# From batch 1 on, Q with K, and V of two heads, by seven block products in place of eight, with column sums taken from exponentials that stay in PSUM

## The reference

```
qkv    = x @ w_qkv                        # 512 -> 3 x 16 heads x 128
scores = q @ k.T / sqrt(128)              # per batch and head, 1024 x 1024
probs  = softmax(scores)                  # over the keys
values = einsum('bhqk,bhkd->bhkd', probs, v)
out    = values @ w_o                     # 2048 -> 512
x      = layernorm(x + out)
x      = layernorm(x + ffn(x))            # routed: 32 experts, 4 per token; and a shared expert
```

## Time and profile before

| | |
|---|---|
| Median of the runs | 2727.69 us |
| Span of the profiled execution (first to last instruction) | 2723.8 us |
| Its own time beside its span | not given by itself; the median is 3.9 us above this span |
| TensorE busy | 2698.9 us, 99% |
| VectorE busy | 2196.8 us, 81% |
| ScalarE busy | 1520.8 us, 56% |
| GpSimd busy | 807.5 us, 30% |
| TensorE's granted clock | 0.999 of full speed |
| Attention | from the start to about 2157 us |

### The profile page before, as it was taken

One profiled execution on the slowest core, in us unless ns is written; L12 is line 12 of the kernel. 1 busy time (PEld: TensorE's weight loads), 2 busy tenths in 40 slices (PEclk: granted clock), 3 DMA queues, 4 the chain that ended last, 5 costly groups with the idle time before them and its releaser, 6 DMA issues.

```text
span 2723.8 us, 41944 instructions
## 1 busy us (share of the span) xinstructions
PE 2698.9 (99%) x12882; PEld 2234.4 (82%) x12882; DVE 2196.8 (81%) x3193; ACT 1520.8 (56%) x2603; POOL 807.5 (30%) x777
## 2 busy tenths in 40 slices
PE   9999999999999999999999999999999999999998
PEld 7888888888888888888888888888887778888887
DVE  6988888889888888898888888988888787433346
ACT  5655555566565566665555657655565532255434
POOL 2222222224222222342222223422221210266621
PEclk9999999999999999999999999999999999999999
DMA  3111111113111111131111112211110231378954
GB/s 120 39 36 38 36 35 35 36 34 116 35 35 35 37 40 35 48 99 37 36 35 35 35 38 66 81 35 42 35 48 14 87 120 43 113 239 254 262 147 155
DMA packets 209640, 193.52 MB, mean 71 GB/s; under 512 B 14620, under 2 KB 162076, under 8 KB 209552
## 3 DMA queue, kind: packets, MB, share of 16 engines
q1 hardware_dynamic: 199056, 180.47, 21.0%
q0 software_dynamic: 10496, 12.02, 2.3%
HBM read 166.41 MB, written 36.18 MB: 74 GB/s over the span
## 4 chain that ended last, share of the span: by engine, by line
PE 94%; DVE 4%; issue 1%; ACT 0%; DMA 0%; POOL 0%; SPq 0%; DVEq 0%; ACTq 0%
PE banks L1828 37%; PE banks L1843 25%; PE banks L1872 13%; PE banks L1750 5%; PE banks L1799 5%; PE banks L1812 3%; PE banks L1759 2%; PE banks L1853 1%; PE banks L1786 1%; DVE colsum L1372 1%; PE banks L1674 0%; PE banks L1727 0%; DVE neg_max L1358 0%; DVE val L1407 0%; DVE raws L1319 0%
## 5 line engine op out<-in xcount | busy, mean ns | idle before, releaser
L1828 PE MATMUL banks<-xt,w_sb 128*128 (+1 forms) x4608 | 1109.2, 390 | 6.5 <-DVE xt L1458 6.5
L1828 PEld LDWEIGHTS banks<-xt,w_sb 128*128 128x128 f32 x4608 | 866.7, 188 | 187.3 <-POOL w_sb L644 6.5
L986 ACT ACTIVATE rows_a<-banks,neg_max 128x1024 f32<-128x1024 f32 x512 | 573.3, 1120 | 700.8 <-DVE neg_max L1358 696.1
L1358 DVE TENSOR_REDUCE neg_max<-banks 128x1 f32<-128x1024 f32 x512 | 625.8, 1222 | 223.6 <-PE banks L1843 212.8
L1843 PE MATMUL banks<-qk 128*128 128x512 f32 x3072 | 779.4, 389 | 0.9 <-ACT rows_a L986 0.8
L1843 PEld LDWEIGHTS banks<-qk 128*128 128x128 f32 x3072 | 576.0, 188 | 122.1 <-ACT rows_a L986 2.6
L1372 DVE SCALAR_TENSOR_TENSOR colsum<-rows_a,inv,colsum 128x1024 f32<-128x1024 f32 x448 | 615.7, 1374 | 17.9
L644 POOL TENSOR_TENSOR w_sb<-raws,w_sb 128x512 fp32r<-128x512 f32 x192 | 249.1, 1297 | 660.4 <-ACT w_sb L926 660.3
L1872 PE MATMUL banks<-wo_sb,val 128*128 128x512 f32 x1536 | 372.2, 391 | 0.2
L1872 PEld LDWEIGHTS banks<-wo_sb,val 128*128 128x128 f32 x1536 | 285.9, 188 | 67.1 <-DVE y_sb L1414 7.9
L655 POOL TENSOR_TENSOR cs<-folded,cs 64x1024 fp32r<-64x1024 f32 x63 | 152.5, 2421 | 406.7 <-ACT cs L967 406.7
(11 more groups left out here) (201 smaller groups left out, 2387.1 us busy)
## 6 DMA issues: line engine op xcount, KB each, us to landing
raws<-in_w_qkv SPq DMA_DIRECT2D x192, 256.0 KB, 2.8
wo_raw<-in_w_o SPq DMA_DIRECT2D x64, 256.0 KB, 2.8
y_sb<-in_x SPq DMA_DIRECT2D x32, 256.0 KB, 3.7
raw_own<-in_w_gate SPq DMA_DIRECT2D x16, 512.0 KB
raw_own<-in_w_up SPq DMA_DIRECT2D x16, 512.0 KB
raw_own<-in_w_down SPq DMA_DIRECT2D x16, 512.0 KB
raws<-in_xT SPq DMA_DIRECT2D x25, 256.0 KB, 3.0
x_wide<-y_sb SPq DMA_DIRECT2D x24, 256.0 KB, 3.6
```

Source lines behind the costliest of these rows:

```text
L986: act.activation(ex[:, t % 2], p_s[:, t % 2], ACT.Exp, bias=neg_max[:, t % 2], accum_out=rowsum[:, t % 2]).then_inc(act_e, 1)
L1358: dve.tensor_reduce(neg_max[:, t % 2], p_s[:, t % 2], AX_X, ALU.max, negate=True)\
L1828: ins = pe.matmul(p_g[:, g % 2], w_sb[:, a, r, c], xt_part(batch_par, b, c, half * NB, NB), start=(c == 0 and (a, b) == PASSES[0]), stop=( ...
```

## The change

**Seven products.** For batches 1 to 3 the projections are taken as products of 2x2 blocks and made by seven block products in place of eight. One such product is a `unit`: 2 chunks x 3 passes = 6 matmuls. Q and K of one head are one such product (7 units, 42 matmuls, in place of 48), and V of two heads is one (42 in place of 48). Four of the seven units run on in one PSUM bank (bank 4 for Q with K); three go into another bank and are combined by ACT (`evac_u`, `evac_v`), VectorE (`add_block`) and GpSimd (`add_v`). Batch 0 is projected as before.

**Blocks from HBM.** The sums of blocks of x and of the weights have to be there in high and low. They are made once, during batch 0 (weights: `sum_t`, `hi_t_sums`, `lo_t`; `store_w`, `store_t`) and during each batch for the next (x: `sum_x`, `hi_x`, `lo_x`, `store_x_step`), written to HBM (`w_jobs`, `x_jobs`) and read back: weights by `load_units` into a ring of seven slots, x by `load_block`.

**Exponentials stay in PSUM.** `exp_here` writes them over the scores. `add_tile` reads them there, and so `scores(t)` waits for `dve_p`, that VectorE has added tile t-2, in place of `act_e`. The SBUF buffers that held them serve as float32 scratch (`e_1`, `u_2`, `e_7`, `v_e1`).

**Who does what.** `lo_val` and the low parts of three of the four Q/K blocks move to GpSimd; splitting weights goes away for batches 1 to 3. `write_x` of the first norm moves from GpSimd to ScalarE for batches 0 to 2. Column sums take two buffers in turn (`colsums`), and the fold stays on VectorE (`fold_here`).

The core of the diff (VectorE's, ScalarE's and TensorE's steps of a pair of heads):

```diff
+        def exp_here(n, t):
+
+            tau = n * T + t
+            on_act.wait_ge(dve_m, tau + 1)
+            on_act.wait_ge(dve_r, tau - 1)
+            act.activation(p_s[:, t % 2], p_s[:, t % 2], ACT.Exp, bias=neg_max[:, t % 2],
+                           accum_out=rowsum[:, t % 2]).then_inc(act_e, 1)
+
...
+        def add_block(i, base, m, which):
+
+            q = m - H
+            pos, bank, to, term = ((P2, 1 if base == 0 else 2, e_1, 1), (P5, 0, e_7, 3), (P4, 1, u_2, 2))[which]
+            on_dve.wait_ge(pe_u, units(i, base + pos))
+            on_dve.wait_ge(act_qe, 3 * q + term)
+            of = psum[:, 4 + bank]
+            if which == 1:
+                tt(to, to, of, ALU.add).then_inc(dve_qc, 1)
+            else:
+                stt(out=to, in0=of, scalar=SCALE, in1=to, op0=ALU.mult, op1=ALU.add).then_inc(dve_qc, 1)
+
...
+        def first_half(b, i):
+            n = 2 * i
+            m = n + 1
+            eighth = isinstance(i, int) and i == PB
+            for t in range(T):
+                if t == 0:
+                    add_y(i - 2, 7 if eighth else 3)
+                if t == 1 and not eighth:
+                    add_y(i - 2, 4)
+                    add_y(i - 2, 5)
+                if t == 2 and not eighth:
+                    add_y(i - 2, 6)
+                    add_y(i - 2, 7)
+                if t == 0:
+                    add_tile(b, n - 1, T - 1, colsums[1], p_s)
+                else:
+                    add_tile(b, n, t - 1, colsums[0], p_s)
+                if t == 2:
+                    add_block(i, 0, m, 0)
+                max_tile(n, t)
+                if t == 0:
+                    fold_here(n - 1, 1)
+                if t == 3:
+                    times_v(0 if eighth else b, n - 1, 1, i - 1)
+                if t == 4:
+                    add_block(i, 0, m, 1)
+                if t == 5:
...
+        def second_half(b, i):
+            n = 2 * i + 1
+            m = n + 1
+            seventh = isinstance(i, int) and i == PB - 1
+            for t in range(T):
+                if t == 0 and seventh:
+                    add_y(i - 1, 2)
+                    add_y(i - 1, 3)
+                if t == 3:
+                    add_block(i, AT_S1, m, 1)
+                if t == 4:
+                    add_block(i, AT_S1, m, 2)
+                    times_v(b, n - 1, 0, i)
+                if t == 0:
+                    add_tile(b, n - 1, T - 1, colsums[0], ex if seventh else p_s)
+                else:
+                    add_tile(b, n, t - 1, colsums[1], p_s)
+                if t >= 5:
+                    add_y(i - 1, t - 1 if seventh else t - 5)
+                max_tile(n, t)
+                if t == 0:
+                    fold_here(n - 1, 0)
+                if t == 1:
+                    add_block(i, AT_S1, m, 0)
+                if t == 4:
+                    lo_block(m, 0)
...
+        def unit(b, i, pos, block, bank, opens):
+
+            on_pe.wait_ge(in_u[RING_OF[pos % 7]], 16 * unit_loads(i, pos))
+            if isinstance(i, int) and i % PB == PB - 1 and pos >= AT_S1:
+                on_pe.wait_ge(in_xb[block], 16 * b)
+            x = xt[:, X_AT[b][block]]
+            for c in range(2):
+                for a, half in PASSES:
+                    ins = pe.matmul(psum[:, bank], w_slot[pos % 7][:, a, c], x[:, half, c],
+                                    start=(opens and c == 0 and (a, half) == PASSES[0]),
+                                    stop=(c == 1 and (a, half) == PASSES[-1]), skip_group_check=True)
+            ins.then_inc(pe_u, 1)
+
...
+        def scores(n, par, t, banked):
 
             if t == 0:
-                on_pe.wait_ge(dve_g, 4 * (n + 1))
-            on_pe.wait_ge(act_e, n * T + t - 1)
+                if banked and not (isinstance(n, int) and n < H):
+                    on_pe.wait_ge(pool_ql, 3 * (n - H + 1))
+                    on_pe.wait_ge(dve_ql, n - H + 1)
+                else:
+                    on_pe.wait_ge(dve_g, 4 * (n + 1))
+            on_pe.wait_ge(dve_p if banked and not (isinstance(n, int) and n == M - 1 and t >= 2) else act_e, n * T + t - 1)
...
+        def first_half(b, i):
+            n = 2 * i
+            eighth = isinstance(i, int) and i == PB
+            for t in range(T):
+                scores(n, 0, t, True)
+                if t < 2 and not eighth:
+                    out_tile(b, i - 2, 4 + 2 * t)
+                    out_tile(b, i - 2, 5 + 2 * t)
+                if t == SPREAD:
+                    on_pe.wait_ge(dve_y, T * (i - 1))
+                    spread(n - 1)
+                for j in {0: (P1,), 1: (P2,), 2: (P6, P7), 3: (P5,), 4: (P4,), 5: (P3,)}.get(t, ()):
+                    qk_unit(b, i, 0, j)
+                if t >= 4:
+                    v_unit(b, i, t - 4)
...
+        def second_half(b, i):
+            n = 2 * i + 1
+            seventh = isinstance(i, int) and i == PB - 1
+            end = isinstance(i, int) and i % PB == PB - 1
+            of = b + 1 if end else b
+            for t in range(T):
+                scores(n, 1, t, True)
+                for j in {0: (P1, P2), 1: (P6, P7), 2: (P5, P4), 3: (P3,)}.get(t, ()):
+                    qk_unit(of, i, 1, j)
+                if t == SPREAD:
+                    if seventh:
+                        on_pe.wait_ge(dve_y, T * (i - 1) + 4)
+                    else:
+                        on_pe.wait_ge(act_ve, evacs(i, 7))
+                    on_pe.wait_ge(dve_qc, 3 * (2 * i + 2 - H) + 1)
+                    spread(n - 1)
+                if 4 <= t < 7:
+                    v_early(of, i, t - 4)
+                if t >= 4:
+                    if t < 6:
+                        on_pe.wait_ge(dve_v, 2 * n)
+                    out_tile(b, i - 1, t if seventh else t - 4)
```

ScalarE's side, in the second pair of heads of a batch (k1), where the first norm's rows are read and written between the exponentials:

```diff
+        def second_half(b, k, i):
+            n = 2 * i + 1
+            m = n + 1
+            k1 = k == 1
+            c = 2 * (b - 1)
+            for t in range(T):
+                if t == 0:
+                    upper_cs(n - 1, colsums[0])
+                if t == 1:
+                    if not (b == 0):
+                        evac_v(i, 6)
+                    evac_u(i, AT_S1 + P1, m, 0)
...
+                if t == 7:
+                    evac_v(i + 1, 2)
+                exp_here(n, t)
+                if k1 and t < 2:
+                    read_x(c + 1, [2 + t])
+                if k1 and t == 1:
+                    write_x(c)
+                if k1 and t == 5:
+                    write_x(c + 1)
```

1142 lines of the change are left out of this document (854 added, 288 removed).

## The result

| | before | after |
|---|---|---|
| Median of the runs, us | 2726.92 (2725.06 to 2727.95) | 2831.39 (2828.43 to 2834.28) |
| Span of the profiled execution | 2723.8 | 2826.9 |
| Mean granted clock of TensorE | 0.999 | 0.987 |

The ratio is 1.0386, with an interval of 1.0371 to 1.0401: 3.9% slower. The prediction had the sign (2764) and not the size: 2831 lies 23 us above the end of its range.

A forecast was written before the change was run, and what follows sets the result against it. VectorE and ScalarE working in turn were to set the pace, hiding TensorE's saving. Ring +7, first norm +21, batch 0 +5 and transfers +3 made +36 on 2723.8: 2760 in the profile, 2764 as median; range 2710 to 2808.

The forecast's parts named there:

- TensorE's saving: Attention projections: 432 of 4608 matmuls go, 97.9 us or 4.08 a pair of heads, hidden under VectorE and ScalarE.
- the ring: VectorE and ScalarE in turn: maximum, exponential, sum, 3.89 us a tile; with extras 66.4 a pair against 66.12, +7 us.
- second head, tile 3: VectorE between maximum and sum: add_block and times_v, 0.6 + 1.2 us, 0.4 more than the room of 1.36.
- ScalarE, late casts: ScalarE between exponentials: its fullest place takes 2.9 us of 2.8, 0.1 late, some 0.3 with what waits.
- all else: Spread-to-spread time outside batch 0 and the second pairs of batches 1 to 3: +9 us of the forecast +36.
- Durations in PSUM: Sum reading PSUM taken as 1.20 us (kept 1.13 and 1.37), exponential writing it as 1.12 (kept 1.07 and 1.25).
- rival C: Sum at 1.13 us and exponential at 1.07 make pairs 64.5 us: 2718 us; chance 0.17.
- The first norm: Second pair of a batch, three times: ScalarE's reads and writes between exponentials cost 7 us each, 21; upper end 12 each.
- Batch 0, the step that failed: First 14 heads: GpSimd's sums of weights and x stretch VectorE's sums; 18 us bare, 5 taken as waiting covers it.
- Transfers: DMA: bandwidth hidden at 109 GB/s a pair; 3 us for three batch ends, without cover 10 each.
- B: TensorE stays the bound, with a tile at 3.6 us in place of 3.89: 2638 us; chance 0.10.
- D: Exponentials in place dearer at 1.25 us (50 us), or transfers late at batch ends (27 us): 2814 us; chance 0.15.

The follow-up runs named there:

- the half sum: Changed kernel with each tile's sum, from batch 1 on, over 512 of its 1024 columns, so no longer a valid layer: 2745.11 us.
- both orders: Changed kernel with, in batch 0, the column sums' low part ahead of sum_t on GpSimd and the weights' load ahead of x's store on SyncE: 2791.26 us.

## Why the prediction was right or wrong

- **TensorE's saving.** Right: 432 matmuls fewer. That it lies hidden under the ring was shown by the half sum (86 us come out). The pace before was read a little short. 33.06 us a head is a mean of 62 distances, and the first of them is 27.66, with 122 matmuls in place of 146. A steady pair took 66.30, not 66.12.
- **The ring.** Right in its mechanism and, but for the last, in its terms: 66.83 us a pair for 66.4. From the starts of VectorE's maxima between 926.82 and 993.65, what a step takes over 3.89:

| term | forecast | measured |
|---|---|---|
| first head, tile 0: fold and two add_y | 1.1 | 1.20 |
| add_block between sum and maximum | 0.6 | 0.59 |
| second head, tile 3 | 0.4 | 0.42 |
| three add_y between sum and maximum | 1.8 | 1.78 |
| ScalarE, late casts | 0.3 | 0.62, in five steps; in two of them the exponential is late |

  What TensorE's idle time is ended by I had wrong: the sum ends almost none of it (1.4 us), ScalarE's `evac_u` and `evac_v` 85 (38.0 + 35.5 + 11.2 in the waits). These stand behind an exponential, and with half a sum the pairs get shorter, so it is the ring all the same.
  That "all else" came out at +9.5 for +9 is partly luck: the ring took more than forecast, and the 3 us for transfers at the ends of the batches did not come.
- **Durations in PSUM.** The exponential in place takes 1087 ns (1118 into SBUF); the sum from PSUM 1284, the same as from SBUF undisturbed. The Trainium skill's rule for ScalarE that the prediction named (PSUM the lower-latency destination) holds, by 31 ns: 0.5 us a pair, too little for rival C. The Trainium skill's page SBUF — State Buffer ("SBUF: two separate sides") says that a VectorE operation with two SBUF inputs and a GpSimd one that reads SBUF exclude each other. The trace agrees: 105 sums with both inputs in SBUF have a mean of 1534 ns and go up to 2390 in batch 0, those with one input in PSUM stay within 1283 to 1286 in all 336 cases, beside a GpSimd that is busy for 27 of 66 us (from 1065 to 1131).
- **The first norm.** The mechanism was right and the size short: 10.4, 9.5 and 9.5 us over a steady pair in place of 7. With the writes away and the queue in order, 3.5 are left for the reads; the prediction's own numbers give 4.1 without the writes (2.5, and 7.0 - 2.6 - 2.8 = 1.6). So the writes cost 6.0 to 6.9, where it had 2.9. The step that held a read, four writes and the split came out at 4.4, 3.6 and 3.6 for 4.2. The other four writes came out at 2.7, 2.6 and 2.6 for 0.3. The prediction asked only when the next exponential comes, and this one is in time; it did not ask what else ScalarE hands to TensorE behind the writes (`evac_v`, and 3.31 us of waiting). The reload of the rows, its upper end ("12 each"), is not what cost this: in the three pairs of the changed kernel none of the four engines that compute waits for a transfer. Such waits came only when the writes had gone to GpSimd.
- **Batch 0, the step that failed.** The prediction put it thus: sums stretched by 0.09 to 0.2 us, "bare it would cost 14 x 1.3 = 18 us. I take 5". The stretch is there, and larger: from 66 to 552 the sums have a mean of 1562 ns after 1373, 0.28 us over an undisturbed one (1285). But the prediction summed what GpSimd does and what this does to VectorE, as if the load were spread evenly. It did not ask in which order GpSimd and SyncE do it. The term was 63.6 us, and the runs with nothing but orders changed took 51 of them away: a load behind six stores, a sum that waits for it, and a split that TensorE waits for queued behind this sum. 59 of the 67 us between forecast and result are this term, 8 the norm.
- **Transfers.** Bandwidth was hidden, as forecast; order was not. The late loads that the experiments moved were late by their place in SyncE's list. The stores of x in runs of 64 words, which no row had shown, stand in that list too. Where SyncE issued a transfer right behind two of them, that issue took 2.5 to 4.2 us in 12 of 12 cases; with 4.6 us or more in between, 0.35 to 0.59, in 12 of 12. The first of the four stores at 314.34 is such a one, 2.66 of the 4.92 us.
- **Rivals.** B and C are out (pairs at 66.84). D's number, 2814, was the nearest, but for neither of its reasons: exponentials in place are cheaper, and the last pairs of a batch take 66.5 us, no more than the others. That it was the nearest is luck.

## What to carry to other kernels

When a change adds work to an engine with time to spare, its share of busy time does not give the cost (GpSimd: 42% with batch 0 at +64 us, 43% with it at +13): write down what stands ahead of each instruction that the bounding engine waits for, on that engine and on the DMA queue. Loads that something waits for go ahead of stores, which wait for results themselves. And in a ring of two engines find the place where one waits for the other: work is free there up to the length of the wait (here 1.36 us), and costs its whole duration two instructions further on.

## What the runs showed of the hardware that I had not expected

- A stall can cost more than its length. After 6.83 us idle the two matmuls of `spread` took 1.01 us and the 12 behind them 4.79, with a granted clock of 0.50 from 326 to 335. After 2.67 us idle (at 721.74 in the changed kernel) 12 took 4.26, with 0.50 from 722 to 724. At full clock (2.4 GHz) 12 take 2.72, all at 1.2 GHz would be twice that. After 1.25 us idle (at 922.36) the clock stayed at 1.00, and 12 took 2.90. With the orders mended the granted clock of the stretch from 66 to 552 us rose from 0.95 to 1.00.
- SyncE's list costs time by itself. The median of its 970 issues in the changed kernel is 0.43 us. Ten stores in a row held a load back by 9.4 us (225.97 to 235.36 with both orders), while the DMA engines were busy for about half the time (0.58 from 66 to 552 us in that run). What an issue right behind two stores of x takes stands above, at the transfers; that the short runs of those stores are the reason was not tested.
